# A masked last tile instead of clearing stores: zero blocks, a third staging buffer and a second queue for the anchor weights

## The reference, cut to what matters

```
scores = sigmoid(x @ gate_weight.T); sc = scores + gate_bias          # 32 experts
... top 2 of 4 groups, then topidx = top 6 experts of each token
routed = sum over 6 of tw * (silu(x @ w_gate[e]) * (x @ w_up[e])) @ w_down[e]      # hidden 128
lg = topidx[:, 0] // 2                                                 # 1 of 16 anchors
anchor = (silu(x @ anchor_w_gate[lg]) * (x @ anchor_w_up[lg])) @ anchor_w_down[lg] # hidden 64
out = routed + shared + 0.1 * anchor;   x = layernorm(x + out)
```

## Time and profile before

| | us |
|---|---|
| runs of the kernel | 1827.92, 1830.91, 1831.14 (median 1830.91) |
| the profiled execution | 1827.43, its span 1825.6 |
| mean granted clock of PE | 0.885 of 2.4 GHz |
| PE busy | 1512.4 (83%) |
| DVE, ACT, POOL busy | 914.7, 538.5, 504.9 |

### The profile page before, as it was taken

How to read it: one execution, slowest core, us unless ns; L and a number is a source line. 1 busy time by engine, 2 the same in 40 slices (tenths; PEclk the granted TensorE clock), 3 DMA queues, 4 the chain that set the end, 5 groups by cost and what they waited for, 6 DMA issues and landing times.

```text
span 1825.6 us, 29467 instructions
## 1 busy us (share of the span) xinstructions
PE 1512.4 (83%) x10007; PEld 1143.4 (63%) x10007; DVE 914.7 (50%) x2498; ACT 538.5 (29%) x1375; POOL 504.9 (28%) x505
## 2 busy tenths in 40 slices
PE   7768987499999995559996998988864779999972
PEld 4455675299999994336654555555642446888861
DVE  7353655421121123998832548686963112566555
ACT  4204443122222220001111344343430112666630
POOL 2020100111111103332231103253635222566653
PEclk9789998599999997679997999999986555999997
DMA  7860000398899881100001011222364763555553
GB/s 207 222 210 24 6 21 14 111 394 330 323 328 332 321 303 43 38 24 1 0 1 29 1 52 63 83 94 70 108 247 159 244 211 109 160 169 168 152 191 150
DMA packets 136003, 260.64 MB, mean 143 GB/s; under 512 B 14511, under 2 KB 108747, under 8 KB 129584
## 3 DMA queue, kind: packets, MB, share of 16 engines
q1 hardware_dynamic: 119104, 218.89, 35.9%
q0 software_dynamic: 16752, 39.88, 6.2%
HBM read 197.31 MB, written 52.73 MB: 137 GB/s over the span
## 4 chain that ended last, share of the span: by engine, by line
PE 46%; DVE 11%; issue 10%; POOL 7%; SPq 4%; DMA 3%; ACT 1%; POOLq 0%; DVEq 0%; ACTq 0%
PE bank L142 42%; POOL xe L1541 3%; PE bank L2032 2%; POOL yr L2150 2%; DVE arena L167 1%; SPq L2162 1%; DMA out_x<-arena 1%; DVE arena L187 1%; SPq L2163 1%; DVE arena L1362 1%; DVE arena L1815 1%; POOL arena L180 1%; PE bank L1052 1%; DVE arena L1805 1%; POOL arena L1270 1%
## 5 line engine op out<-in xcount | busy, mean ns | idle before, releaser
L142 PE MATMUL bank<-arena 128*128 128x128 f32 (+10 forms) x8682 | 1361.2, 344 | 171.8 <-issue 22.4
L142 PEld LDWEIGHTS bank<-arena 128*128 128x128 f32 (+5 forms) x8682 | 999.9, 184 | 485.8 <-issue 315.4
L2150 POOL DMA_INDIRECT yr<-arena x158 | 157.5, 997 | 183.7 <-ACT arena L2087 115.3
L180 POOL TENSOR_TENSOR arena<-arena 128x1 f32<-128x1 f32 (+1 forms) x64 | 54.4, 850 | 513.4 <-DVE arena L172 513.3
L1085 DVE TENSOR_SCALAR arena<-bank,arena 128x128 f32<-128x128 f32 x188 | 52.9, 344 | 271.7 <-PE bank L142 271.7
L1541 POOL DMA_INDIRECT xe<-arena x112 | 113.1, 1010 | 57.4 <-issue 30.9
L1104 POOL DMA_INDIRECT arena<-xd,arena x47 | 44.6, 950 | 294.0 <-PE bank L1052 260.1
L2107 DVE COPY arena<-arena 128x768 f32 x127 | 73.0, 575 | 67.2 <-issue 67.2
L2032 PE MATMUL bank<-arena 128*128 128x128 f32 x316 | 71.0, 311 | 33.1 <-DMA arena<-xe 33.0
L2087 ACT ACTIVATE arena<-bank,arena 128x256 f32<-128x256 f32 x158 | 75.0, 475 | 71.7 <-PE bank L142 65.4
L1719 ACT ACTIVATE arena<-bank,arena 128x256 f32<-128x256 f32 x128 | 59.0, 473 | 98.2 <-DVE arena L1805 98.2
(11 more groups left out here) (237 smaller groups left out, 1336.3 us busy)
## 6 DMA issues: line engine op xcount, KB each, us to landing
arena<-in_bank SPq DMA_DIRECT2D x47, 2052.0 KB
arena<-xe SPq DMA_DIRECT2D x158, 129.0 KB
arena<-kd SPq DMA_DIRECT2D x16, 1024.0 KB, 10.9
arena<-arena SPq DMA_DIRECT2D x16, 896.0 KB, 5.4
arena<-in_bank SPq DMA_DIRECT2D x8, 1536.0 KB, 9.4
arena<-yr SPq DMA_DIRECT2D x16, 768.0 KB, 14.6
arena<-in_banka SPq DMA_DIRECT2D x31, 256.0 KB, 2.9
xe<-arena SPq DMA_DIRECT2D x50, 129.0 KB, 3.2
```

The source lines that it names most:

```text
L142: return t.matmul(o, l, r, start=start, stop=stop, skip_group_check=True)
L180: p.tensor_tensor(st[:, 40:40 + nb], st[:, 32:32 + nb], cc("mhalf", 0, nb), ALU.pow).then_inc(rstd, 1)
L2150: p.indirect_dma_start(yr, bass.IndirectOffsetOnAxis(ap=sidx.bitcast(I32)[:, n:n + 1], axis=0), y2_ring[n % NY], None, bounds_check=14335, ...
```

## The change

- `xe` is filled from the second block of each region on (constant `base`), and one DMA in the second stage writes a zero block in front of each of the 48 regions and one behind the last. All `clear` are gone.
- The last tile of a region is no longer the block in which its last row lies: its 128 rows end with the region's last row. It so repeats rows of the tile before (or zeros of the first block). `e1` to `e3` compute the number of repeated rows as well, and the mask `dupm` adds to the code of a repeated row so much that it is out of bounds. The lists hold row numbers (`rowA`, `rowE`) now. This costs one more transpose and two more small matmuls on PE and some small operations on DVE.
- Unit 7 has a third staging buffer, so its staging waits for no scatter. Scatters of unit 5 from its fifth on move behind all other work of POOL's second stage, then come six of unit 6, two of unit 7 (anchors), and the other eight and twelve.
- The first four expert weight loads (groups 0, 3, 4, 5) follow the staging of unit 7, no longer ahead of it; the other four follow the row loads of the anchor tiles 8, 14, 22 and 28.
- Anchor weights of odd tiles are loaded from ACT's queue (`wl` in `steps_g`), of even ones from SP's.

```diff
-REGION = 818 * 128
+REGION = 817 * 128
-        stg = [alloc(14 * RW) for _ in range(2)]
+        stg = [alloc(14 * RW) for _ in range(2)] + [arena[:, marks[3]:marks[3] + 14 * RW]]
+        def held_in(u):
+            return (2, 0) if u == 7 else (u % 2, u // 2)
...
-                        if u[:2] != "sx" or n < 6:
+                        if u[:2] != "sx" or i < 32:
...
-                    for blk in (544, 817):
-                        s.dma_start(xe[blk * 128:(blk + 1) * 128, :], zero).then_inc(cleared, 16)
+                    s.dma_start(bass.AP(tensor=xe.tensor, offset=0, ap=[[RW, 128], [17 * 128 * RW, 49], [1, RW]]), view(zero, 0, [[0, 49], [1, RW]])).then_inc(cleared, 16)
...
             for n in range(2, 8):
-                if n == 7:
-                    b, k = U["ow2", 15]
-                    s.wait_ge(bank_full[b], k + 1)
-                    for i in range(4):
-                        load_experts(s, i)
                 stage_rows(s, n)
+            for i in (0, 3, 4, 5):
+                load_experts(s, i)
...
+            for u, js in ((5, range(4, 14)), (6, range(6)), (7, range(2)), (6, range(6, 14)), (7, range(2, 14))):
+                scatter_rows(p, u, js)
...
+                for key, NT, at, exp, row, dup, E, zb in (("tilesA", ...), ("tiles", ...)):   # vector_ends, e3
+                    v.tensor_scalar(exp.bitcast(I32)[:, 0:NT], banks[b][:, 0:NT], float(E - 1), None, ALU.min)
+                    v.scalar_tensor_tensor(rowf[:, 0:NT], banks[b][:, at:at + NT], zb - 17.0 * E + 1.0, cc("iota", 0, NT), ALU.add, ALU.add)
+                    v.tensor_scalar(dup, banks[b][:, 2 * at:2 * at + NT], cc("part"), 1.0 * FAR, ALU.is_gt, ALU.mult)
+                    v.tensor_scalar(rowf[:, 0:NT], rowf[:, 0:NT], float(zb), 128.0, ALU.min, ALU.mult)
+                    v.tensor_scalar(dup, dup, 1.0 * FAR, None, ALU.add)
+                    v.tensor_tensor(row.bitcast(I32)[:, 0:NT], rowf[:, 0:NT], banks[b][:, 2 * at:2 * at + NT], ALU.subtract)
+                    v.engine_nop().then_inc(tiled, 1)
...
+                if u == "wl" and n % 2:                                   # scalar_experts
+                    load_anchor(a, n)
...
+        def load_anchor(e, n):
+            if n >= 6:
+                b, k = U["dn", n - 6]
+                e.wait_ge(bank_full[b], k + 1)
+            at = e.value_load(expA.bitcast(I32)[0:1, n:n + 1], min_val=0, max_val=15)
+            e.dma_start(a_ring[n % 6], ins["banka"][bass.ds(at * 128, 128), :]).then_inc(a_land[n % 6], 16)
...
-            for e in range(32, 48):                                       # sync_experts
-                clear(e)
...
+            late = {8: 6, 14: 7, 22: 1, 28: 2}
             for n in range(NTA + NT1):
...
+                    if n % 2 == 0:
+                        load_anchor(s, n)
+                    at = s.value_load(rowA.bitcast(I32)[0:1, n:n + 1], min_val=0, max_val=816 * 128)
...
-                if 3 <= n < NTA:
-                    if n % 4 == 3 and loaded < 8:
-                        load_experts(s, loaded)
-                        loaded += 1
-                    for _ in range(2):
-                        if cleared_to < 32:
-                            clear(cleared_to)
-                            cleared_to += 1
+                if n in late:
+                    if late[n] in (1, 2):
+                        s.wait_ge(rows_out[2], 16 * 12)
+                        s.wait_ge(an_rows_out[2], 16 * 2)
+                    load_experts(s, late[n])
```

More of the change, by code:

```diff
@@ L1446, in build @@
         run = [alloc(48) for _ in range(2)]
-        posi = [alloc(16).bitcast(I32) for _ in range(2)]
+        posi = [alloc(16).bitcast(I32) for _ in range(3)]
         tw, twn = alloc(16), alloc(16)
         tri16b, ones16b = alloc(64).bitcast(F16), alloc(64).bitcast(F16)
-        fin, runi = alloc(96), alloc(48)
+        fin = alloc(144)
         zero = alloc(272)[:, 0:RW]
@@ L1456, in build @@
             sem(n) for n in ("chosen", "placed", "zeroed", "cleared", "fixed", "wb_in"))
-        rows_out, staged = [sem(f"rows_out{i}") for i in range(2)], [sem(f"staged{i}") for i in range(2)]
-        an_rows_out = [sem(f"an_rows_out{i}") for i in range(2)]
+        rows_out, staged = [sem(f"rows_out{i}") for i in range(3)], [sem(f"staged{i}") for i in range(3)]
+        an_rows_out = [sem(f"an_rows_out{i}") for i in range(3)]
+        def held_in(u):
+            return (2, 0) if u == 7 else (u % 2, u // 2)
         def steps_f():
@@ L1535, in scatter_rows @@
         def scatter_rows(p, u, js):
[L1537 removed]
+            i, n = held_in(u)
+            p.wait_ge(staged[i], 32 * (n + 1))
             p.wait_ge(placed, 2 * (u + 1))
@@ L1684, in tensor_second @@
                     t.transpose(banks[b][0:48, 0:128], fin[:, 0:48], ident)
-                    t.transpose(banks[b][0:48, 128:256], fin[:, 48:96], ident).then_inc(bank_full[b], 1)
+                    t.transpose(banks[b][0:48, 128:256], fin[:, 48:96], ident)
+                    t.transpose(banks[b][0:48, 256:384], fin[:, 96:144], ident).then_inc(bank_full[b], 1)
                 elif u == "e3":
@@ L2010, in steps_g @@
             for n in range(NTA + NT1 + 9):
-                for u, d in (("dn", 7), ("mu", 6), ("gu", 5), ("cw", 4), ("tr", 3), ("ga", 0), ("sc", 8)):
+                for u, d in (("dn", 7), ("mu", 6), ("gu", 5), ("cw", 4), ("tr", 3), ("wl", 1), ("sc", 8)):
                     i = n - d
-                    if 0 <= i < NTA + NT1 and (u != "cw" or i >= NTA):
+                    if 0 <= i < NTA + NT1 and (u != "cw" or i >= NTA) and (u != "wl" or i < NTA):
                         yield u, i
@@ L2065, in scalar_experts @@
         def scalar_experts(a):
+            a.wait_ge(tiled, 1)
             for u, n in steps_g():
                 I = 64 if n < NTA else 128
-                if u == "tr" and I == 128:
+                if u == "wl" and n % 2:
+                    load_anchor(a, n)
+                elif u == "tr" and I == 128:
                     if n >= 3:
@@ L2141, in gpsimd_experts @@
         def gpsimd_experts(p):
-            for u in (6, 7):
-                scatter_rows(p, u, range(2))
-            for u in (6, 7):
-                scatter_rows(p, u, range(2, 14))
             for u, n in steps_g():
@@ L2331, in constants @@
     e = np.arange(48)
-    put("base", 128.0 * (17 * e + (e >= 32))[None, :])
+    put("base", 128.0 * (17 * e + 1)[None, :])
     put("scanm", (e != 32)[None, :])
```

111 lines of the change are left out of this document (53 added, 58 removed).

## The result

The changed kernel takes 1798.76 us (median of 4 runs, 1797.37 to 1800.32) where the kernel before takes 1829.99 beside it (1827.92 to 1831.14): 0.9831 of it [0.9814, 0.9848], 31 us less. 1802 was forecast. The profiled execution took 1799.82 us with a span of 1797.9, 27.7 less than the span before.

What follows compares the result with a forecast made beforehand. SP's issue list, then PE at 1.2 GHz, were taken to bound the anchor part, and PE the expert tiles. Terms -27.1, +2.7 and -2.4 made -26.8: 1800.6 us profiled, 1802 as median; range 1783 to 1816.

Steps and rivals of the forecast that it cites:

- The sum: Whole kernel: 26.8 us less, so 1800.6 us for the profiled execution and 1802 as the median.
- The start: Start of the experts stage: without clearing stores, first load at 1398.5 and tile 0 transposed at 1403.4, -7.5 us.
- The pace: Anchor tiles from tile 4: SP's list no longer binds, PE at 1.2 GHz does, 3.67 us a tile.
- at a pace near 2.8 us: Anchor tiles up to tile 9: a risen clock gives this pace, -3.5 us at three chances in four, -2.4 on average.
- rival (a): Anchor part: clock rises and stays up, loop of loads bounds at 2.9 us a tile, about 1781 us; chance 0.12.
- Late weight loads: Expert loads at anchor tiles 8, 14, 22, 28: 0 to 1.8 us each, +2.7 us for three at half.
- rival (b): Anchor part: late weight loads still stall PE, up to 1822 us, about 1813 if stalls are half; chance 0.17.
- The signs of being wrong: Anchor part long at clock 1.00, row waits over 2 us behind tiles 8, 14, 22 or 28, second stage ending later.
- The second queue: Anchor weights split over SP and ACT: saves issue time only, worth about nothing; ACT's issue taken as 1.16 us, hidden.
- Behind the anchor part: Expert tiles after tile 31: bound by PE, stretch unchanged near 285 us, masked code operation costing 0.
- The zero transfer: 49 zero blocks sent in the second stage: 18 to 31 us, hidden by some 20 us of cover, landed before 1030.
- rival (c): Second stage: zero transfer takes 157 us and delays the context of group 1, 1912 us in all; chance 0.04.

Runs made afterwards that it cites:

- e6: Changed kernel with all anchor weights on SP's queue and two 129 KB zero stores behind the rows of each of tiles 3 to 18; 1815.05 us, 0.9928 of before.
- e2: Changed kernel with all anchor weights loaded from SP's queue; 1840.27 us on a slower chip, 0.9775 of before.
- e10: Same edit as e2, run again in another group on a slower chip; 1839.62 us, 0.9749 of before.
- e7: Changed kernel with the loads of e4 and four unneeded 512-column matmuls ahead of tile 0; 1754.48 us, 0.9621 of before.
- e5: Changed kernel with the row code operation moved from DVE to ACT; 1790.09 us, 0.9791 of before.
- e3: Changed kernel with expert weight groups 6 and 7 loaded before the anchor tiles; 1835.67 us on a slower chip, 0.9731 of before.
- e1: Kernel before, with a column in place of the constant in the code operation of `mu`; 1882.76 us on a slower chip, 0.9983 of before.
- e9: Same edit as e1, run again in another group on a slower chip; 1878.88 us, 0.9955 of before.
- e8: e7 with the row code operation moved to ACT as in e5; 1836.77 us on a slower chip, 0.9745 of before.
- e4: e3 with groups 1 and 2 as eight 384 KB loads behind odd tiles 15 to 29; 1826.88 us on a slower chip, 0.9710 of before.
- e11: Same edit as e4, run again in another group on a slower chip; 1839.91 us, 0.9772 of before.
- e0: The changed kernel unedited, run again as the measure for its group; 1798.94 us, 0.9836 of before.

## Why the prediction was right, and where its steps were off

**The sum** was right: 1802 against 1798.76, and 1800.6 against 1799.82 for the profiled execution. Its terms were off by several us each, +3.0 at the start, -6.0 in the anchor part and +2.1 behind it, and nearly cancelled: that it came within 1 us is luck, that it came within the range is not.

**The start, forecast -7.5, measured -4.5.** The first load went out 0.84 us after the list (the list's last row begins at 1398.65 and takes 0.19), as forecast. But the second stage came 1.9 us later, whose cause stays open, and from the first load to tile 0's transposes it took 6.66 us, not 4.92: +1.7, where "some tenths" were given to the scatters beside it. The list itself came 0.7 sooner than forecast, against its own stage (1398.84 less 1.89 is 1396.95, not 1397.6).

**The pace, 3.67 us from tile 4 on.** It was exact from tile 9 on, 22 tiles in 80.67 us, and e6 shows by the way back that it was SP's list, stores and all weights, that had hidden it; e2 and e10 leave the stores as its main part. Ahead of tile 9 the pace was better than forecast: tile 0 to tile 9 took 23.9 us where 27.2 was the mean of the forecast (11.2, 5 times 3.67, less 2.4). The clock rose at 1410.3, tile 2, and with it a tile took 2.0 us. The step that failed is "at a pace near 2.8 us", with rival (a)'s bound by the loop of loads, 2.9 a tile. It divided the 5.8 us from `dn` of n-6 to the landed rows by two tiles. In PE's list `dn` of n-6 stands right behind the transposes of n-3, so the 5.8 us and some 0.4 for that `dn` are spread over three tiles: an estimate of 2.1 each. The trace has this for tile 8: transposes of tile 5 at 1415.20, its rows issued at 1418.12, its transposes at 1421.89, 6.69 us for three tiles with the one wait of 0.58 in them. SP's own 3.4 us a pair, 1.7 a tile, bounds less. e7 ran 31 tiles at 2.01 but for its short waits.

**Late weight loads, forecast +2.7, measured 0** for those of tiles 14, 22 and 28; full (6.26) for that of tile 8, as in the earlier trace rows. PE's lag behind SP covers them, where PE is at 1.2 GHz: the rows of tile 15 were issued 8.9 us before PE wanted them, as forecast. The step that failed for tile 8 is the same lag. The tiles ahead of it ran at 2.0 us, so its next rows were issued at 1419.82 and wanted at 1423.96, 4.1 us later. Where the lag is gone the others show too: e5, with the clock up, waits 4.72 us behind the load at tile 22, e6 behind the one at tile 14, and e7 at loads a quarter the size. So rival (b) was right at one load of four.

**The signs of being wrong.** Two of the three that the prediction named came: rows were waited for by more than 2 us behind the load at tile 8, and the second stage ended later than before.

**Rival (a), the clock that stays up**, did not come in the changed kernel, but its mechanism was right and the forecast named the obstacle: "loads at 8 are the first thing to stop it". In e7 it was worth more than the 21 us that it was given, as its tiles take 2.0 us and not 2.9.

**Rule and row on the clock.** The granted clock was 0.50 for 80.66 us of PE without idle time here, for 118.67 us in e3, and 1.00 for the same tiles in e7. The Trainium skill, "TensorE: Matmul & The Clock Gate", section "What's actually happening", says that sustained activity releases the throttle. e7 agrees that activity keeps it released; the changed kernel and e3 show anchor tiles not releasing it in their 80.66 and 118.67 us.

**The second queue** was forecast at nothing; e2 and e10 agree as far as their scatter goes. ACT's issues are 1.36 us apart instead of 1.16, and hidden.

**Behind the anchor part, forecast 0, measured +2.1.** This step was wrong in two of its sentences: that the 127 expert tiles are bound by PE, and that the masked code operation, "at the same size", costs 0. The operation on a column takes 0.207 us instead of 0.145, and 119 expert tiles took 195.00 us (last row of the windows above) where the trace before has 119 in 191.00. Groups on DVE by line in that window (busy us, mean ns, idle before and its cause):

```profile
L2123 DVE COPY arena<-arena 128x768 f32 x119 | 67.0, 563 | 60.7 <-issue 60.7
L2131 DVE TENSOR_TENSOR arena<-bank,arena 128x128 f32<-128x128 f32 x119 | 34.7, 292 | 12.8 <-DVE arena L2126 0.5
L2126 DVE TENSOR_SCALAR arena<-arena 128x1 int32<-128x1 f32 x118 | 24.4, 207 | 0.0
L2134 DVE TENSOR_TENSOR arena<-arena 128x256 f32<-128x256 f32 x16 | 6.7, 419 | 0.0
```

Busy time makes DVE look free (62% of the window), but each copy of weights has 0.5 us of "issue" ahead of it, for the register with the expert's number: 0.56 + 0.51 + 0.29 + 0.21 is 1.57 us of a typical tile of 1.56, and at tiles with an addition of an anchor result (+0.42) it is DVE alone that decides, 1.90 against 1.84 before (the addition overlaps its neighbours by some 0.1). e5 takes the operation off DVE and gets 8.0 us back in 121 tiles, more than the 4 that it had cost, since before the change DVE was a part of the bound as well. That DVE bounds the tiles with an addition is shown by e5; in the others (1.52 us on DVE before, 1.56 after, 1.55 in e5) it does so hardly, as PE without a wait takes 1.54 (e5). That the column lengthens DVE's step by 0.05 to 0.06 us is shown by the traces of e1 and e9; that this makes all of the 4.0 us is argued, as their times could not show it. The other 2 us go the other way: the clock rose 12.1 us behind tile 31's transposes, not 14.6.

**The zero transfer** took 26.1 us of the 18 to 31 forecast, and was hidden; rival (c) and its 157 us are out. Unit 7's buffer and the moved scatters changed nothing that the trace shows.

## What to carry to other kernels

A stall can cost more than its length: look at the clock before and after it. Here the clock fell in one wait of 6 us, and the 22 anchor tiles behind it ran at half speed; e7, without that wait and with work ahead of the stage, took 45 us less. Put large transfers where nothing small and urgent is queued behind them, and try work ahead of a stage that brings the clock up (it came up and stayed in e7, not in e8). And where an engine's busy share is low, add the "issue" time that stands between its own instructions before calling another engine the bound; an operation as small as one column counts there.

## What the runs showed of the hardware

- Tiles of the same kind run at 1.2 or at 2.4 GHz for a whole stage: 80.66 us and 118.67 us (e3) at 0.50 without idle time, and 64.48 us at 1.00 with 5.1 us of idle time in pieces (the longest of the marked ones 1.30).
- The clock could rise in the middle of such tiles, at 1442.1 in e5, 1513 in e4, 1511.5 in e11 and 1521.8 in e8. No cause was found.
- It fell in waits of PE of 3.6 to 6.6 us, or less than 1 us behind them (before, changed, e0, e2, e10, e5), and in e5, e6 and e8 behind waits of 1.64, 2.34 and 2.1 us; in e7 five waits of 0.4 to 1.3 us left it up.
- The same 128x1 operation on DVE takes 0.144 us with a constant and 0.206 with a column as operand; on ACT 0.284.
- A register load ahead of a copy on DVE shows as 0.48 to 0.51 us of "issue", not as busy time.
- Rows of 129 KB issued 1.3 us after a load of 1536 KB on the same queue landed 10.4 us after their issue; behind 384 KB pieces they made PE wait 1.3 us at most.
- 49 blocks of 129 KB go out as one transfer in 26.1 us, from one issue of 0.43 us.
- Some chips run the whole kernel some 3% slower (1887.5 and 1885.9 against 1829.3 for the kernel before), with long tails in the durations of tiles; nothing in the kernels explains it.
